# Keys of the second attention spread by ScalarE, one semaphore for the spent score tiles, values in 32-column strips ahead of the weighed values

## What is computed

```python
q = (query @ Wq.T + bq).reshape(B, T, H, D).transpose(0, 2, 1, 3)
k = (key @ Wk.T + bk).reshape(B, S, H, D).transpose(0, 2, 1, 3)
v = (value @ Wv.T + bv).reshape(B, S, H, D).transpose(0, 2, 1, 3)
scores = jnp.einsum('bhtd,bhsd->bhts', q, k) / np.sqrt(D)
scores = scores + causal[None, None]
attn = jax.nn.softmax(scores, axis=-1)
out = jnp.einsum('bhts,bhsd->bhtd', attn, v)
out = out.transpose(0, 2, 1, 3).reshape(B, T, E) @ Wo.T + bo
```

## Time and profile before

| | us |
|---|---|
| median of 3 runs | 864.5 |
| lowest, highest | 860.74, 865.0 |
| the profiled execution, device time | 864.41 |
| its span in the trace | 862.3 |
| PE busy | 814.8 (94%) |
| DVE busy | 630.6 (73%) |
| ACT busy | 566.0 (66%) |
| POOL busy | 287.1 (33%) |

### The profile page before, as it was taken

One profiled execution on the slowest core, in us unless ns is written; L12 is line 12 of the kernel. 1 busy time (PEld: TensorE's weight loads), 2 busy tenths in 40 slices (PEclk: granted clock), 3 DMA queues, 4 the chain that ended last, 5 costly groups with the idle time before them and its releaser, 6 DMA issues.

```text
span 862.3 us, 20490 instructions
## 1 busy us (share of the span) xinstructions
PE 814.8 (94%) x7364; PEld 569.8 (66%) x7364; DVE 630.6 (73%) x1587; ACT 566.0 (66%) x1597; POOL 287.1 (33%) x587
## 2 busy tenths in 40 slices
PE   8999999999999999999999899999899989899986
PEld 8887888888889986644444444444466755676652
DVE  5677777677776665676785847765989867889876
ACT  3666667767777766786546466456467779777664
POOL 4355445444454443210000000002156620334455
PEclk9999999999999999999999999999999999999999
DMA  8700000000000000000000000000000000000000
GB/s 335 162 2 2 1 2 2 2 2 1 2 1 2 2 1 2 1 1 0 1 1 0 1 1 0 1 0 1 1 28 3 4 3 1 3 3 3 3 15 37
DMA packets 7887, 13.54 MB, mean 16 GB/s; under 512 B 4342, under 2 KB 5100, under 8 KB 7532
## 3 DMA queue, kind: packets, MB, share of 16 engines
q1 hardware_dynamic: 7788, 12.24, 4.5%
HBM read 11.19 MB, written 1.05 MB: 14 GB/s over the span
## 4 chain that ended last, share of the span: by engine, by line
PE 60%; DVE 17%; POOL 10%; issue 6%; ACT 6%; DMA 1%; DVEq 0%; POOLq 0%; SPq 0%; ACTq 0%
PE psum L1561 10%; PE psum L772 6%; POOL rstd L520 4%; PE psum L812 4%; PE psum L755 3%; DVE arena L2119 3%; PE psum L1547 3%; PE psum L764 3%; POOL arena L1100 2%; PE psum L1570 2%; DVE negmax L1010 2%; PE psum L840 2%; PE psum L2014 2%; PE psum L790 2%; ACT arena L910 2%
## 5 line engine op out<-in xcount | busy, mean ns | idle before, releaser
L517 POOL TENSOR_TENSOR ve<-mv,epsv 128x1 f32<-128x1 f32 x176 | 36.3, 206 | 459.0 <-DVE mv L512 459.0
L1561 PE MATMUL psum<-arena,w1f 128*128 128x512 f32 x240 | 109.5, 592 | 0.0
L520 POOL TENSOR_TENSOR rstd<-ve,epsv 128x1 f32<-128x1 f32 x176 | 101.4, 576 | 13.8
L910 ACT ACTIVATE arena<-psum,negmax 128x128 f32<-128x128 f32 x256 | 90.6, 408 | 22.1 <-DVE negmax L1010 22.1
L1561 PEld LDWEIGHTS psum<-arena,w1f 128*128 128x128 f32 x240 | 45.5, 190 | 48.9 <-issue 45.0
L1100 POOL TENSOR_TENSOR arena<-arena,rsum 128x512 f32<-128x512 f32 x64 | 65.2, 1039 | 5.6 <-DVE rsum L1016 5.6
L910 ACT ACTIVATION_READ_ACCUMULATOR arena<-psum,negmax 128x1 f32 x256 | 63.4, 248 | 0.0
L1010 DVE TENSOR_REDUCE negmax<-psum 128x8 f32<-128x1024 f32 x32 | 39.2, 1225 | 32.9 <-PE psum L812 32.9
L755 PE MATMUL psum<-arena,sclA 128*128 128x128 f32 x512 | 62.5, 275 | 0.1
L772 PE MATMUL psum<-arena 128*128 128x512 f32 x128 | 61.3, 598 | 0.7 <-DVE arena L1005 0.4
L840 PE MATMUL psum<-prjB,arena 128*128 128x128 f32 x512 | 59.9, 275 | 0.0
(11 more groups left out here) (376 smaller groups left out, 1980.1 us busy)
## 6 DMA issues: line engine op xcount, KB each, us to landing
w<-in_w0qk SPq DMA_DIRECT2D x2, 512.0 KB, 5.0
w<-in_w0vo SPq DMA_DIRECT2D x1, 1024.0 KB, 7.6
cT<-in_cT SPq DMA_DIRECT2D x1, 1024.0 KB, 15.8
out<-x_tok SPq DMA_DIRECT2D x4, 256.0 KB, 2.2
rows<-in_rows SPq DMA_DIRECT2D x1, 836.0 KB, 13.1
x_tok<-in_x_tok SPq DMA_DIRECT2D x1, 768.0 KB, 9.8
ctx_tok<-in_ctx_tok SPq DMA_DIRECT2D x1, 768.0 KB, 11.0
wa<-in_wa SPq DMA_DIRECT2D x1, 768.0 KB, 17.1
```

What stands on the lines that cost most here:

```text
L520: pool.tensor_tensor(rstd[:, u, self.i:self.i + 1], ve[:, u, self.i:self.i + 1], epsv[:, 1:2], ALU.pow) \
L910: m = nc.scalar.activation(e0[:, b, g, :], ps(k, P, j * P), ACT.Exp, bias=negmax0[:, b, g:g + 1], accum_out=sum0[:, b, g:g + 1])
L1561: nc.tensor.matmul(ps(k), w1("e2", j * 384 + arg * D, j * 384 + (arg + 1) * D), f1_Hm[:, n, 2 * j + i, :], start=False, stop=False)
```

## The change

1. POOL's km is gone. ACT spreads the keys: for each of the four head groups one instruction from PSUM with the group's mask as scale and its masked bias (`bk2`, built once on DVE), instead of one instruction to `kT2`. The scores no longer wait for `spread`.
2. The s job of DVE raises one semaphore, `spent`, and stands for nothing; the four score matmuls of tile n wait for `spent` n, and ACT's exponential waits for it too. After the last tile alone DVE waits and raises all four banks by 16. This holds for both attentions that use the function.
3. The values of the second attention are formed in eight matmuls of 32 output columns instead of four of 64.
4. In `ATT_PE`, av stands right behind v instead of behind out. In `DRAIN_PE`, v of tile 15 stands ahead of av of tile 14. No bank is changed (`DRAIN_BANKS` had av of tile 14 in bank 1).
5. "ou" of tiles 12 and 15 stands behind the feed-forward's F instead of behind its masks.

```diff
-        ATT_PE = [("s", 4), ("lnt", 9), ("v", 5), ("ot", 7), ("t", 5), ("out", 7), ("av", 6), ("qk", 2), ("lnt0", 1)]
+        ATT_PE = [("s", 4), ("lnt", 9), ("v", 5), ("av", 6), ("ot", 7), ("t", 5), ("out", 7), ("qk", 2), ("lnt0", 1)]
-        ATT_POOL = [("root", 0), ("km", 2), ("tail", 7), ("bias", 8), ("own", 1)]
+        ATT_POOL = [("root", 0), ("tail", 7), ("bias", 8), ("own", 1)]
-        DRAIN_PE = [("lnt", 11), ("K", 0), ("av", 14), ("ot", 13), ("v", 15), ("t", 15), ("out", 13), ("lnt", 12), ("ot", 14), ("av", 15), ("out", 14),
+        DRAIN_PE = [("lnt", 11), ("K", 0), ("v", 15), ("av", 14), ("ot", 13), ("t", 15), ("out", 13), ("lnt", 12), ("ot", 14), ("av", 15), ("out", 14),
...
-            at = {"pe": [(("H", 1), "pt", old), (("H", 2) if new[1] else ("M", "B0"), "att", old), (("F", *of_old, None) if new[1] else ("M", "AB"), "ou", old), (("B", BETA), "l2", old),
+            at = {"pe": [(("H", 1), "pt", old), (("H", 2) if new[1] else ("M", "B0"), "att", old), (("F", *of_old, None), "ou", old), (("B", BETA), "l2", old),
...
-                        fill(pe, a, f"s{i}", t)
+                        if t.n == 0:
+                            fill(pe, a, f"s{i}", t)
+                        else:
+                            pe.wait_ge(spent, t.n)
...
-                    else:
-                        pe.wait_ge(spread, t.times(1, 1))
...
-                        for r in range(2):
-                            w = wgt(n, "v").rearrange("p (g q c) -> p g q c", q=2, c=DH2)[:, :, r, :]
-                            m = nc.tensor.matmul(psum[r * S:(r + 1) * S, k, b * S:(b + 1) * S], cT[:, t.n * P + b * S:t.n * P + (b + 1) * S],
-                                                 w, start=True, stop=True)
+                        for i in range(4):
+                            w = wgt(n, "v").rearrange("p (g q c) -> p g q c", q=2, c=DH2)[:, :, i // 2, :]
+                            x = t.n * P + b * S + i % 2 * 32
+                            m = nc.tensor.matmul(psum[i * 32:(i + 1) * 32, k, b * S:(b + 1) * S], cT[:, x:x + 32], w, start=True, stop=True)
...
-                        nc.scalar.activation(kT2[:, u, :], ps(k, P, P), ACT.Identity, bias=vec("a2_bk"))
+                        if t.n == 0:
+                            act.wait_ge(a_half, 4)
+                        for h in range(QUAD):
+                            nc.scalar.activation(km[:, u, :, h, :], ps(k, P, P).rearrange("p (b k) -> p b k", b=2), ACT.Identity,
+                                                 bias=bk2[:, h:h + 1], scale=head4[:, h:h + 1])
...
-                    for i in range(4):
-                        stored(act, a, f"s{i}", t)
+                    act.wait_ge(spent, t.times(1, 1))
...
-                        .then_inc(free[0], 1)
-                    stored(dve, a, "s0", t)
-                    for i in range(1, 4):
-                        dve.sem_inc(free[i], 1)
+                        .then_inc(spent, 1)
+                    if t.n == TILES - 1:
+                        dve.wait_ge(spent, TILES)
+                        for i in range(4):
+                            dve.sem_inc(free[i], TILES)
```

More of the change, by code:

```diff
@@ L1294, in build @@
                    ("max", 1), ("s", 1), ("own", 5), of_prev("Z"), of_last("G"), ("apply", 5), of_last("Z")]
-        POOL_END = [("root", 0), ("root", 1), ("own", 0), ("own", 1), ("root", 2), ("root", 3), ("own", 2), ("own", 3), ("root", 4), ("own", 4), ("km", 0), ("km", 1),
-                    ("km", 2), ("root", 5), ("own", 5), ("km", 3)]
+        POOL_END = [("root", 0), ("root", 1), ("own", 0), ("own", 1), ("root", 2), ("root", 3), ("own", 2), ("own", 3), ("root", 4), ("own", 4), ("root", 5), ("own", 5)]
         END_BANKS = {("ha1A", PREV): 7, ("ha1B", PREV): 5, ("f21", PREV): 4, ("hh1", LAST): 5, ("f110", LAST): 6, ("f111", LAST): 7,
@@ L1901, in build @@
         bk3 = sb("bk3", [P, QUAD])
+        bk2 = sb("bk2", [P, QUAD])
         v3_built = sem("v3_built")
@@ L1959, in attention @@
             max2 = carve(2 * H2).rearrange("p (u h) -> p u h", u=2)
-            kT2 = carve(2 * P).rearrange("p (u k) -> p u k", u=2) if late else None
             assert used["n"] <= (24 * C1 if late else ARENA - (2 * 2 * HALF * 18 + HALF + QUAD)), used
-            spread, maxed, exped, inverted = (sem(f"a{n}_{x}") for x in ("spread", "max", "exp", "rsum"))
+            maxed, exped, inverted, spent = (sem(f"a{n}_{x}") for x in ("max", "exp", "rsum", "spent"))
             def on_pe(pe, kind, n_tile):
@@ L2149, in on_pool @@
                     before.root(pool, t)
-                if kind == "km":
-                    u = t.n % 2
-                    stored(pool, a, "qk", t)
-                    if t.n == 0:
-                        pool.wait_ge(a_half, 2 * (n - 1))
-                    if t.n >= 2:
-                        filled(pool, a, "s3", t - 2)
-                    pool.tensor_tensor(km[:, u, :, :, :], kT2[:, u, :].rearrange("p (b k) -> p b k", b=2).unsqueeze(2).to_broadcast((P, 2, QUAD, S)),
-                                       head4.unsqueeze(1).unsqueeze(3).to_broadcast((P, 2, QUAD, S)), ALU.mult).then_inc(spread, 1)
                 if kind == "tail":
@@ L2178, in dve_build @@
                 nc.vector.tensor_scalar(bk3[:, :], head4, vec("a3_bk"), None, ALU.mult).then_inc(a_half, 1)
+                nc.vector.tensor_scalar(bk2[:, :], head4, vec("a2_bk"), None, ALU.mult).then_inc(a_half, 1)
                 nc.vector.tensor_copy(Vx.rearrange("p u g (r c) -> p (u g) r c", c=9)[:, :, :, DH2],
```

## The result

| | before | after |
|---|---|---|
| median, us | 864.75 (4 runs) | 887.18 (4 runs) |
| lowest, highest | 860.74, 867.47 | 883.25, 889.86 |
| the profiled execution | 864.41 | 886.4 |
| its span | 862.3 | 884.3 |

The changed kernel is slower: ratio 1.0261, 95% interval 1.0231 to 1.0292. The forecast was 880.5 us, with a range of 870 to 890, and slower.

The account below looks back on a forecast made before the run. The prediction took PE and DVE to run a ring with almost no slack, 4.875 us a step in the second attention. Its terms, 19.75 + 0.4 - 0.4 - 3.6 = +16.1, on 864.4 gave 880.5 us, range 870 to 890.

Parts of the forecast that it names:

- Which circle rules: Second attention: the longer of two loops of waits, the one over ACT, sets the pace, 6.41 us a step against 4.875.
- The twelve intervals: Second attention, masks of tile 3 to tile 15: 16.9 us for 11 intervals, 1.05 for the last, 1.8 first; together 19.75.
- The 1.8 for a first step: First step of the second attention: v to t takes longer and ACT is late; 1.2 to 2.0 us, taken 1.8.
- circle A: Second attention, loop over PE and DVE: v, its copy, av, ot, t, out, add, subtraction, masks; 5.92 us a step.
- The warm-up: Tiles ahead of the second attention's steps: qk of tile 1 waits longer for bank 7; 0 to 0.8 us, taken 0.4.
- The drain: End of the second attention: v of tile 15 ahead of av of tile 14, no stall, t sooner; -0.4 us.
- The last attention: It only gets `spent`, which removes DVE's 0.33 us behind each subtraction; -3.6 us, ends 0 and -6.6.
- ou: Job moved behind the feed-forward's F: the wait for DVE's L1085 passes to the next job; zero, ends -1 to +1.
- circle B: Second attention, loop over ACT, whose copy of v stands behind keys, queries, turned input, exponential, turned output; 6.41 us a step.
- ACT keeps up: Rival, second attention: circle A rules, as key instructions are cheaper or ACT made up time; +10.2, 874.6 us; 15 in 100.
- the clock falls: Rival, second attention: granted clock 1.2 instead of 2.4 GHz, PE's parts of the circle double; +30, 910 us; 4 in 100.
- it works as built: Rival, second attention: av's wait on bank 6 costs nothing, PE's step falls to about 4.5 us; 856 us; 4 in 100.

Follow-up runs that it names:

- e3: The kernel before with the semaphore `spent` alone, keys still on POOL and av behind out: 859.72 us, ratio to before 0.996.
- e11: The kernel before with `spent`, DVE's apply moved behind max, and v in eight 32-column matmuls in its old place: 857.10 us, ratio to before 0.995.
- e2: The changed kernel with av back behind out and the old `DRAIN_PE` order, keys still on ACT: 871.34 us, ratio to before 1.008.
- e1: The changed kernel with the keys spread by POOL again, av still right behind v: 874.69 us, ratio to before 1.012.
- e9: The kernel before with `spent`, DVE's apply moved behind max, and ou moved behind the feed-forward's F: 856.46 us, ratio to before 0.992.
- e10: The kernel before with `spent`, apply moved, v in strips behind av (bank 4), ot in bank 6, exponential between queries and turned input: 858.73 us, ratio 0.995.

## Why the prediction was right, and where it was off

**Which circle rules** was right, and so was most of its sum. Measured from one copy of v to the next (667.58 to 674.34): copy and hand-over 0.63, av 0.67, ot to the add 1.47 (forecast 1.45), add to qk 0.34, qk to the keys 0.75, keys 1.39, queries and turned input 0.40, exponential 0.95, turned output 0.16, in all 6.76 against the 6.41 forecast. 0.31 of the 0.35 is one term, "**four of these instead of one, at the pitch of 657.04 to 657.31, 4 x 0.27 = 1.08**". Four of L2092 took 1.39, 0.347 each. The groups of ACT (mean ns) of before and of the change show why:

```profile
L2089 ACT ACTIVATE arena<-psum,vecs 128x128 f32<-128x128 f32 x10 | 3.7, 368 | 9.8 <-PE psum L2044 9.8
```

```profile
L2092 ACT ACTIVATE arena<-psum,bk,arena 128x128 f32<-128x128 f32 x36 | 13.6, 456 | 6.0 <-PE psum L2044 6.0
```

The new instruction takes a vector as scale besides the vector as bias, and lasts 88 ns longer. It also writes its result in two pieces of 64, but that is not the reason: the trace of before has two instructions of 128x128 with both vectors, L964 in such pieces at 457 ns and L646 in one piece at 463. The Trainium skill states this ("ScalarE: Activation LUTs", What ACT_TABLE_LOAD costs): each pointer operand adds about 93 ns. The traces agree: 276 ns without a vector (L649), 368 with one, 457 with two. L964 in the groups of ACT, and in the timeline it has a pitch of 0.34 (204.46 to 204.80):

```profile
L964 ACT ACTIVATE arena<-psum,vecs 128x128 f32<-128x128 f32 x16 | 7.3, 457 | 0.0
```

So the price stood in the trace of before; the prediction had taken an instruction of the same tile for one of the same form.

**The twelve intervals** came to +21.93, where the terms gave 19.75. Eleven times the 0.35 is 3.85 more. The 1.8 for a first step on top of the circles did not appear: the first two intervals, 6.36 and 6.60 us, are even 0.56 shorter than the steady 6.76. The last two are 0.67 longer than the terms have them (6.99 and 6.36 us instead of 6.76 and circle A's 5.92). 3.85 - 1.8 - 0.56 + 0.67 is the 2.2 that is missing, so about half of what the 0.35 would have cost was hidden by a term that was too large.

**The warm-up**, "**0 to 0.8, taken 0.4**", was +2.34. With three more key instructions for each tile, qk of tile 1 waits for bank 7 longer, and DVE's chain doesn't cover it; behind that wait the granted clock was 0.57 from 612 to 616 us. PE in the change:

```profile
611.02 0.49 PE L2042 MATMUL psum<-cT,wa 128*128 128x128 f32 x2 [1.85 <-ACT arena L2094]
```

Before, this wait was 0.72, so it explains 1.13 of the 2.34. From the masks behind it to the feed-forward's L1583 (L1584 before), PE takes 4.16 us instead of 3.04, which is another 1.1 and goes by the clock: the ten transposes L268, for one, last 2.23 us instead of 1.38.

**The drain**, "**so there is no stall ... -0.4**", was +2.30. Of this 2.26 lies between the masks of tile 15 and L1909, the first matmuls of the next attention's keys (6.35 us instead of 4.09): one more wait of av for the copy of v (0.69 at 714.53), which the count of intervals up to tile 15's masks left out, a wait of 0.33 for ACT's copy of the transposes, and about 1.3 for the stretch from 714 to 718 us at a granted clock of 0.57, where the eight transposes took 1.91 us instead of 1.04. And there is a stall at the moved v of tile 15. The bank of av of tile 14 is another, but v itself needs bank 6, which av of tile 13 still holds until DVE has read it:

```profile
720.85 0.43 PE L2000 MATMUL psum<-wa,cT 128*32 128x64 f32 x16 [1.27 <-DVE arena L2145]
```

From L1909 to the turn L639 of tile 12 it is 4.51 us for 4.46 before, with a pause of 0.86 inside av of tile 14 (up to 697.89) in the place of this wait. The moved v gave nothing, instead of the 0.4.

**The last attention** was forecast at -3.6 and gave -3.03; the mechanism was right. Behind the subtraction DVE no longer stands, which answers to the earlier trace rows; the change's DVE:

```profile
767.87 1.22 DVE L2122 TENSOR_TENSOR arena<-psum,arena 128x1024 f32<-128x1024 f32 x1
769.00 0.34 DVE L578 SCALAR_TENSOR_TENSOR x_tok<-psum,small,x_tok 128x128 f32<-128x128 f32 x1
```

e3, which has `spent` alone, takes 3.55 us less than before in all, 1.1 of it from the twelve intervals of the second attention (58.50 less 57.42).

**"ou"** was right: the wait passed to the next job, and what is left is 0.35 to 0.5 us. The -3.62 us ahead of the second attention are not its doing. e11, with ou in its old place and no piece of lower clock there, has a later mark (L1524, the turn's first group with a wait for L1622) at 501.53, the change at 501.22 (L1523) and before at 504.85.

**What the prediction didn't see** is the third circle. It priced the keys on ACT as "**most of it in circle B already**", and called `spent` and the end of km worth nothing only because circle A covers DVE. e2 shows that these keys cost about 11.6 us (871.34 to e3's 859.72) even with av in its old place, and e1 that av's move costs 15.0 with the keys on POOL. Together, 26.6, they are nearly the whole difference between the change and e3 (about 26, from the ratios 1.0261 and 0.996), so neither hides the other; both comparisons also hold the strips and the moved ou, which e11 and e9 show to be small. The rival "ACT keeps up" (874.6) describes e1, whose keys are not on ACT, and that it does so to 0.1 us is luck, since before takes 1.5 us less on e1's chip.

**The clock.** The rival "the clock falls" had the whole stage at the lower level. The steady steps stayed at 1.00, but the two short falls at the stage's ends cost 1.1 and 1.3 us. The evidence against it was picked too narrowly: behind the other "ou" in the same trace of before, at 488.64 with a wait of 1.85 us, the granted clock from 488 to 496 us is 0.79. The rival "it works as built" priced a change of shape at 0.20 us, by the difference of two rows; e10 has about 0.1 for each.

**The sum** came out 5.9 us low in the profiled execution (886.4 to 880.5). Against the terms it is 1.9 in the warm-up, 2.2 in the twelve intervals, 2.7 in the drain, 0.6 in the last attention and 2.1 behind it, less 3.6 for what before lost ahead of 610 us, mostly to its two pieces of lower clock. That these offset the change's own three pieces (about 1.1, 1.3 and 1.7) is luck. So the right mechanism gave a sum that is about a quarter too small.

## What to carry to other kernels

Where each engine takes its work in order, a moved instruction is to be priced by the circles that it closes, all of them: go round from each wait back to itself, over every engine, and add what stands in each queue between. Work handed to an engine with pauses is not free if something that another engine waits for stands behind it in that queue; here three more key instructions (1.04 us) ahead of the exponential cost 0.92 us a step (e2's 5.74 beside e3's 4.82). An instruction is to be priced by a row of the same form, with the same operands, and not only of the same size. And putting one shape side by side, which saves PE about 0.20 us a step, pays only where the neighbour doesn't need the result of an evacuation that has just begun.
